# Routed experts: split rows turned beside the tokens, and the halves of the down weights made at other places in the loop

## The reference, cut to what matters

```python
x = x + attention(layernorm(x))              # 2 x 1024 tokens of 512, 32 heads, 8 of keys and values
flat = layernorm(x).reshape(2048, 512)
scores = softmax(flat @ router_w)            # 64 experts; the top 4 by logits + router_bias, weights normed
g = silu(einsum('nd,edf->nef', flat, wg))    # wg, wu: [64, 512, 128]
u = einsum('nd,edf->nef', flat, wu)
routed = einsum('ne,nef,efd->nd', comb, g * u, wd)                            # wd: [64, 128, 512]
shared = einsum('nsh,shd->nd', silu(flat @ swg) * (flat @ swu), swd)          # 2 shared experts of 512
x = x + (routed + shared)
```

## Time and profile before

| | |
|---|---|
| median of 3 runs | 1113.19 us (1111.9 to 1113.76) |
| the profiled execution | 1116.51 us, span 1114.7 us |
| busy share of the span | PE 95%, PEld 45%, DVE 77%, ACT 58%, POOL 49% |
| mean granted TensorE clock | 0.994 of full speed |
| DMA | 150.66 MB over the queues, 135 GB/s over the span |

### The profile page before, as it was taken

How to read it: one execution, slowest core, us unless ns; L and a number is a source line. 1 busy time by engine, 2 the same in 40 slices (tenths; PEclk the granted TensorE clock), 3 DMA queues, 4 the chain that set the end, 5 groups by cost and what they waited for, 6 DMA issues and landing times.

```text
span 1114.7 us, 29689 instructions
## 1 busy us (share of the span) xinstructions
PE 1063.6 (95%) x9832; PEld 497.5 (45%) x9833; DVE 858.0 (77%) x1331; ACT 651.2 (58%) x1334; POOL 548.1 (49%) x540
## 2 busy tenths in 40 slices
PE   5998899999999998899999999999999999999998
PEld 3533333333333333355444555555554555544443
DVE  6986999999999994697889546666675666758373
ACT  3323788888888889444512156666765667632020
POOL 6621333343334334347846838888885688720000
PEclk9998999999999999999999999999999999999999
DMA  8163111211121120244000458778775678549261
GB/s 254 36 167 92 45 45 45 75 54 43 54 73 45 44 64 3 77 152 152 1 1 1 162 185 279 248 251 288 276 260 181 205 278 296 190 155 279 87 227 38
DMA packets 72409, 150.66 MB, mean 135 GB/s; under 512 B 19460, under 2 KB 20868, under 8 KB 72356
## 3 DMA queue, kind: packets, MB, share of 16 engines
q1 hardware_dynamic: 52404, 109.51, 31.1%
q0 software_dynamic: 18304, 38.86, 10.5%
q10 hardware_dynamic: 1648, 1.58, 0.4%
HBM read 223.90 MB, written 38.80 MB: 236 GB/s over the span
## 4 chain that ended last, share of the span: by engine, by line
PE 71%; DVE 16%; issue 7%; ACT 3%; DMA 1%; POOL 1%; another core or an unknown queue 0%; DVEq 0%; SPq 0%; ACTq 0%; POOLq 0%
PE PS L1480 15%; PE PS L1357 13%; PE PS L1462 7%; PE PS L1499 6%; PE PS L1271 6%; DVE maxes L1554 6%; PE PS L1152 4%; PE PS L1220 4%; DVE max_low L1554 4%; PE PS L1249 3%; PE PS L1440 3%; ACT att L1004 2%; PE PS L1324 2%; PE PS L1441 2%; PE PS L1489 1%
## 5 line engine op out<-in xcount | busy, mean ns | idle before, releaser
L1004 ACT ACTIVATE att<-PS 128x512 f32<-128x512 f32 x576 | 312.5, 595 | 50.9 <-PE PS L1249 44.1
L1271 PE MATMUL PS<-att,v_head 128*32 128x256 f32 (+1 forms) x2560 | 178.2, 369 | 0.9 <-POOL att L793 0.9
L1554 DVE TENSOR_REDUCE maxes<-PS 128x2 f32<-128x1024 f32 (+2 forms) x192 | 173.5, 946 | 1.2 <-PE PS L1157 1.1
L1357 PE MATMUL PS<-XN,att 128*128 128x512 f16 x768 | 167.1, 379 | 0.3 <-ACT w_att L1066 0.3
L1554 DVE TENSOR_REDUCE max_low<-PS 128x2 f32<-128x1024 f32 x128 | 153.8, 1213 | 4.9 <-PE PS L1152 3.0
L793 POOL TENSOR_SCALAR_AFFINE_SELECT att<-att 128x512 f32<-128x512 f32 (+1 forms) x96 | 74.9, 787 | 127.7 <-ACT att L1004 126.9
L919 POOL DMA_INDIRECT w_att<-xn_rows,idx x96 | 98.9, 1030 | 57.9 <-ACT idx L1097 30.5
L1249 PE MATMUL PS<-att 50*128 50x512 f16 (+1 forms) x640 | 111.7, 362 | 14.1 <-ACT att L1004 11.7
L1152 PE MATMUL PS<-att 48*128 48x512 f16 (+7 forms) x768 | 115.6, 325 | 9.0 <-DVE max_low L1554 3.9
L1357 PEld LDWEIGHTS PS<-XN,att 128*128 128x128 f16 x768 | 74.7, 98 | 90.2 <-issue 0.8
L1062 ACT ACTIVATE w_att<-PS 128x512 f32<-128x512 f32 x32 | 19.1, 598 | 157.3 <-PE PS L1357 157.3
(11 more groups left out here) (205 smaller groups left out, 1818.9 us busy)
## 6 DMA issues: line engine op xcount, KB each, us to landing
ring<-in_L_ffn_wg_dram SPq DMA_DIRECT2D x96, 512.0 KB
XT<-in_L_ffn_wg_dram SPq DMA_DIRECT2D x96, 512.0 KB
ring<-in_L_ffn_wd_dram SPq DMA_DIRECT2D x96, 256.0 KB
XT<-in_L_ffn_wd_dram SPq DMA_DIRECT2D x96, 256.0 KB
ring<-choice_y SPq DMA_DIRECT2D x16, 1024.0 KB, 6.2
att<-q_stacks SPq DMA_DIRECT2D x60, 128.0 KB, 2.5
xn_rows<-ring SPq DMA_DIRECT2D x16, 256.0 KB, 3.1
out_dram<-X SPq DMA_DIRECT2D x16, 256.0 KB, 6.2
```

Of the source, the lines that this page charges most:

```text
L1004: act.activation(probs[:, n0 % RING, u * BANK:(u + 1) * BANK], bank((2 * n0 + u) % EXP_BANKS), ACT.Exp, scale=HD ** -0.5 / QK_SCALE ** 2). ...
L1271: mm = pe.matmul(PS[32 * r:32 * r + 32, at:at + qn], v_head[b][:, kt, :], probs[:, (NS * b + s) % RING, a:a + qn], start=s in (0, NS0), st ...
L1357: mm = pe.matmul(bank(2 * (n % 2) + k), shared_w[:, 2 * k + w, C * s + c, at:at + P], v[:, c, tokens], start=(c == 0 and w == 0 and v is x ...
L1554: last = dve.reduce_max(out, src, AXX)
```

## The change

Three orders are changed; no instruction is added or dropped.

- TensorE turns the hidden rows of pair n-2, no longer those of n-1. It does so right behind the token turn and in front of `expert_up`, no longer between `expert_up` and `expert_down`.
- ScalarE copies those rows out right behind the tokens. The high half of the down weights of n-1, no longer of n, is made in front of the silu, no longer at the end of the step. The index of a later gather goes behind the copy of the hidden rows.
- VectorE makes the low half of the down weights (still of n-1) behind the hidden product and in front of `e_low`, no longer behind the result.

The steps that are left over are done behind the loop.

```diff
@@ ScalarE, expert_pairs
                     if not (last and j == JP - 1):
                         turned_tokens(n + 1, j + 1)
-                        if not last:
-                            next_tokens(i + 1 + (j + 1) // JP, (j + 1) % JP)
+                    if not (first and j < 2):
+                        hidden_turned(n - 2, (j - 2) % JP)
+                    if not last:
+                        next_tokens(i + 1 + (j + 1) // JP, (j + 1) % JP)
+                    if not (first and j < 1):
+                        down_high(n - 1, (j - 1) % JP, i if j else i - 1)
                     silu(n, j)
                     e_high(n, j)
-                    if not (first and j < 1):
-                        hidden_turned(n - 1, (j - 1) % JP)
-                    down_high(n, j, i)
@@ behind the loop
+            hidden_turned(PAIRS - 2, JP - 2)
             hidden_turned(PAIRS - 1, JP - 1)
+            down_high(PAIRS - 1, JP - 1, LANE_TILES - 1)
@@ TensorE, expert_pairs
                         turn_slots(n + 1, j + 1, i)
+                    if not (first and j < 2):
+                        turn_hidden(n - 2, (j - 2) % JP)
                     expert_up(n, j, i)
-                    if not (first and j < 1):
-                        turn_hidden(n - 1, (j - 1) % JP)
                     if not (first and j < 2):
                         expert_down(n - 2, (j - 2) % JP)
@@ behind the loop
+            turn_hidden(PAIRS - 2, JP - 2)
             turn_hidden(PAIRS - 1, JP - 1)
             expert_down(PAIRS - 2, JP - 2)
@@ VectorE, expert_pairs
                     expert_hidden(n, j)
+                    if not (first and j < 1):
+                        down_low(n - 1, (j - 1) % JP)
                     e_low(n, j)
                     if not (first and j < 2):
                         expert_y(n - 2, (j - 2) % JP, i if j >= 2 else i - 1)
-                    if not (first and j < 1):
-                        down_low(n - 1, (j - 1) % JP)
```

## The result

The changed kernel takes 1092.01 us (median of 5 runs, 1091.38 to 1092.99) beside 1112.41 us before: 20.4 us less, ratio 0.9815 (95% interval 0.98 to 0.9829). The forecast was 1093.8 us, a gain of 19.4 counted from 1113.2, the median of the three runs of before that were known then. The profiled execution took 1091.62 us with a span of 1089.8.

What follows compares the result with a forecast made beforehand. TensorE's routed loop was taken as the bound: 92 steps saving 0.22 us each (20.2 us), less 0.8 behind the loop, took 1113.2 to 1093.8 us. The range was 1088.5 to 1102.5 us.

Steps and rivals of the forecast that it cites:

- TensorE's loop bounds the kernel; a step loses two changes of shape: Routed loop: grouping both turns cuts a step from 3.43 to 3.22 us; 0.22 taken for 92 steps, 20.2 us.
- three places of before: TensorE's old rows: leaving down costs 0.10, leaving up 0.09, two wide matmuls 0.22 between narrow ones against 0.10 grouped.
- data type: Up to down: fp32 followed by f16 keeps the 0.09 price, 0.12 less a step, 1103.0 us; chance 0.10.
- the token turn's 0.32: Upper bound per step: the share of the token turn's 0.72 us put down to shape changes, were it the hidden turn's price.
- The work arrives in time: Other engines in the loop keep up with the shorter step; the silu would be 0.1 us late, harmlessly.
- Stalls as they are, plus or minus 3: Routed loop: the 7.2 us of stalls read from the profile stay, plus or minus 3 us.
- 0.8 us behind the loop: After the loop: down of 95 starts 5.2 us behind the last up instead of 4.4, adding 0.8 us.
- Sum: Whole kernel: -20.2 + 0.8 = -19.4 us, from a median of 1113.2 to 1093.8 us.
- Another engine takes part of the gain: Loop: ScalarE with a late load, or more stalled steps, lose half the gain, 1098 to 1107 us; chance 0.12.
- GpSimd at its limit: Loop: GpSimd's period stays at 3.43 us, so no change, 1113.5 us; chance 0.03 together with the gather hold.
- The hold of `down_low` by a gather: VectorE: `down_low` started during a gather waits until it ends, step 3.4 again, 1113.5 us; chance 0.01.
- Late weights: Loop: loads asked for sooner come late in most iterations, 18 us slower, 1131 us; chance 0.04.

Runs made afterwards that it cites:

- wide_between: The changed kernel with one added 128x128 matmul in each down, between up and down: 1118.29 us, ratio 1.0053 to the kernel before.
- turn_only: The kernel before with only the hidden turn and its copy moved, both halves of the down weights left in place: 1107.78 us, ratio 0.995.
- second profile of before: The unchanged kernel before, profiled once more: 1112.21 us, span 1110.4.
- narrow_between: The changed kernel with one product added between up and down as two 128x64 matmuls: 1098.34 us, ratio 0.9874 to the kernel before.
- swap: The kernel before with one edit, TensorE turning the hidden rows of n-1 behind down instead of in front of it: 1105.52 us, ratio 0.9932.
- swap_low: The kernel before with hidden turn behind down, low half before `e_low`, `e_low` first in the last step: 1160.3 us beside 1122.9; again 1163.8 beside 1123.1.
- tail: The changed kernel with `e_low` of 95 before the last step's `down_low`, and last `down_high` before both `hidden_turned` behind the loop: 1091.11 us, ratio 0.9809.

## Why the prediction was right, by its steps

- **TensorE's loop bounds the kernel; a step loses two changes of shape.** Right. 3.21 for 3.22 us; 0.225 for 0.22 in each of 92 steps, 20.7 us. The three stretches agree within 0.02. The prices that were read at three places of before (0.10, 0.09, 0.12) lie about those of wide_between (0.10 and 0.11). The bound for a data type and that of the token turn's 0.32 were both off.
- **The work arrives in time.** Right for the change as a whole. ScalarE's last item ends 1.91 behind up's start (forecast 2.1), the silu isn't late, VectorE and GpSimd keep up. What the prediction did not see is how much hung on it: it put down the move of the low half as worth nothing, with "Down of n-2 finds its low half made a step earlier", and priced no rival in which that fails. turn_only shows that rival at work: without this move the gain is 5.7 us, not 20.
- **Stalls as they are, plus or minus 3.** Right by luck. The 7.2 us were read from one execution that was 4 us above the median; in the second profile of before they are 1.7, and 0.1 after. The 3.4 us put down to the place around 850 us were too few as well: the two steps there took 5.36 and 6.57 us, 5.1 over the regular ones, since the stretched matmuls of an up count as busy. The prediction was made against the execution's own time and carried over as a difference, so the error didn't enter.
- **0.8 us behind the loop.** The start of the last down was right: 5.1 behind the last up, for 4.4 before and a forecast of 5.2. In time it may be less: the shared experts begin 6.5 behind the end of the last up, and 6.0 in the second profile of before. In both the clock falls in the hole (0.83 over 10 us, which is 1.7 us of the full clock and has no term in the forecast); the first profile of before hadn't that, with 5.2.
- **Sum.** 20.7 for the steps, 1.6 for the stalls, less 0.5 behind the loop and 0.6 in front of it (first hidden turn at 654.5 and 653.9) is 21.2, where the spans differ by 1110.4 - 1089.8 = 20.6 and the medians by 20.4. The forecast had 20.2 - 0.8.
- **The rivals.** The data type: refuted (narrow_between). Another engine takes part of the gain: it does in turn_only and swap, not in the change. GpSimd at its limit: refuted, it follows at 3.21. The hold of `down_low` by a gather: refuted, `down_low` began inside a gather 55 times and inside a scatter 39 times in the changed kernel, and lasted 1.22 or 1.23. The section of the Trainium skill that the prediction names for it, "SBUF — State Buffer", SBUF: two separate sides, makes its rule for two SBUF inputs depend on a GpSimd operation that reads SBUF, which the prediction left out; with the measurement the other way, the measurement decides. Late weights: not in this kernel.

## What to carry to other kernels

Read the shape column of TensorE's rows: where groups of 128x128 and 128x64 matmuls alternate, each change cost 0.11 us here, twice as much as a matmul of 128 columns (0.055), and the place to save it is the order of the groups, not their work. A faster bound engine needs the next chain shortened in the same edit: here the new order alone gave a quarter, the halves' move nothing, and both together everything, so test parts of a change in pairs before dropping one. Profile the kernel before twice when its profiled execution stands off its median.

## What the hardware showed that was not expected

- ScalarE and TensorE can stand still together for 3 to 4.4 us in a stretch in which SyncE issues weight loads, with no wait for an instruction of this core in the profile: once in the first profile of before, not in the second, and in about every third step of swap_low. The cause is open.
- The same hole behind the loop is followed by a fallen clock in some executions and not in others. In the changed kernel TensorE was idle for 1.91 us in front of the last down, and the granted clock was 0.83 over 10 us (0.50, the lower of its two levels, from 960 to 962.5). In wide_between it was idle for 1.86 and the clock stayed at 1.00. The kernel before had 1.55 in both profiles, and the clock fell in the second alone; in tail it fell with 0.95 as the longest. What decides it isn't shown.
- GpSimd's indirect DMAs are held by VectorE's `down_low` whichever of them starts in it. In most steps of the change's first two thirds it is the scatter (1.48 in place of 1.02), in the last third the gather (1.49 to 1.67 in place of 1.03) while the scatter takes its 1.02. The step is the same.
